# Keys and outputs of a scan turned by VectorE through memory scratch instead of by TensorE, in a gated scan-and-experts kernel

## The reference, cut to what is computed

```python
# x, ctx: (16, 256, 512)
k = layernorm(x); v = ctx
# per channel c, over the 256 steps of each of 16 sequences:
#   y_t = (e1*aa + e2*v_t) / (e1*bb + e2);  aa, bb decayed by exp(-exp(time_decay)), then exp(k_t)*v_t, exp(k_t) added
x = x + tanh(g_xattn) * y
h = layernorm(x)                                  # 4096 tokens
routed = two of eight experts per token (I=352), capacity 1280 rows each, weighted by the softmax of their two logits
shared = (silu(h @ Wg) * (h @ Wu)) @ Wd           # inner width 1408
x = x + tanh(g_ffn) * (routed + shared)
```

## Time and profile before

| | us |
|---|---|
| median of 3 runs | 1230.34 |
| lowest, highest | 1228.75, 1232.13 |
| the profiled execution | 1232.66 |
| its span, first to last instruction | 1230.9 |

### The profile page before, as it was taken

How to read it: one execution, slowest core, us unless ns; L and a number is a source line. 1 busy time by engine, 2 the same in 40 slices (tenths; PEclk the granted TensorE clock), 3 DMA queues, 4 the chain that set the end, 5 groups by cost and what they waited for, 6 DMA issues and landing times. The chain is left out here.

```text
span 1230.9 us, 25978 instructions
## 1 busy us (share of the span) xinstructions
PE 1163.2 (94%) x8396; PEld 817.2 (66%) x8396; DVE 682.7 (55%) x1357; ACT 509.6 (41%) x915; POOL 653.7 (53%) x754
## 2 busy tenths in 40 slices
PE   1478999999999999999999989999999999999998
PEld 1366777777777777777776767566666666666653
DVE  6776787786786777776777866222222223222112
ACT  5665444443544443544534443333333333333220
POOL 7887457367457457456557542344444444444320
PEclk9998999999999999999999989999999999999999
DMA  8373232232222222222332323999899989997738
GB/s 234 92 206 72 53 70 53 53 69 52 54 66 52 60 61 55 68 49 60 87 69 48 59 65 62 204 178 180 173 169 172 176 171 165 178 169 130 127 50 319
DMA packets 232773, 136.29 MB, mean 111 GB/s; under 512 B 176477, under 2 KB 201077, under 8 KB 232544
## 3 DMA queue, kind: packets, MB, share of 16 engines
q1 hardware_dynamic: 213792, 97.55, 34.3%
q0 software_dynamic: 18048, 37.47, 17.6%
q10 hardware_dynamic: 832, 0.02, 0.0%
HBM read 69.83 MB, written 44.97 MB: 93 GB/s over the span
## 5 line engine op out<-in xcount | busy, mean ns | idle before, releaser
L1024 PE MATMUL PU<-xT,wreg 128*128 128x256 f16 x4224 | 504.5, 276 | 0.4 <-DVE srng L1311 0.4
L1024 PEld LDWEIGHTS PU<-xT,wreg 128*128 128x128 f16 x4224 | 415.1, 99 | 74.8 <-DVE srng L1311 0.7
L753 POOL DMA_INDIRECT moe_d<-wkv,acc x71 | 112.0, 1578 | 217.2 <-ACT wkv L928 214.2
L1131 PE MATMUL PU<-acc,wkv 128*128 x1284 | 214.5, 312 | 0.0
L1057 PE MATMUL PD<-wreg,hreg 128*128 128x512 f16 x858 | 206.4, 379 | 0.0
L634 POOL TENSOR_TENSOR hreg<-srng,hreg 128x256 f16<-128x256 f32 x165 | 134.6, 822 | 73.9 <-ACT hreg L850 72.9
L1131 PEld LDWEIGHTS PU<-acc,wkv 128*128 128x128 f16 x1284 | 125.1, 97 | 69.4
L1545 DVE TENSOR_TENSOR wkv<-PR,wkv 128x384 f16<-128x384 f32 x71 | 39.6, 557 | 208.1 <-ACT wkv L922 148.7
L1152 PE MATMUL PD<-acc,wkv 128*128 (+1 forms) x639 | 149.6, 379 | 1.5 <-DVE wkv L1545 1.5
L834 ACT ACTIVATE srng<-PU 128x256 f32<-128x256 f32 x176 | 66.7, 379 | 201.4 <-PE PU L1024 149.5
L1057 PEld LDWEIGHTS PD<-wreg,hreg 128*128 128x128 f16 x858 | 84.0, 98 | 73.5
(11 more groups left out here) (177 smaller groups left out, 1327.5 us busy)
## 6 DMA issues: line engine op xcount, KB each, us to landing
wreg<-in_L_ffn_w_up_gate SPq DMA_DIRECT2D x48, 176.0 KB
acc<-in_x SPq DMA_DIRECT2D x32, 256.0 KB, 3.0
xhl_d<-wkv SPq DMA_DIRECT2D x32, 256.0 KB, 2.3
wkv<-in_ctx SPq DMA_DIRECT2D x112, 64.0 KB, 2.4
moe_d<-acc SPq DMA_DIRECT2D x13, 512.0 KB
out<-moe_d SPq DMA_DIRECT2D x2, 3328.0 KB, 21.1
acc<-n_L_ffn_shared_w_up_gate SPq DMA_DIRECT2D x16, 256.0 KB, 5.7
wreg<-in_L_ffn_w_down SPq DMA_DIRECT2D x12, 256.0 KB
```

Source lines behind the costliest of these rows:

```text
L753: pool.indirect_dma_start(out=moe_d, out_offset=bass.IndirectOffsetOnAxis(ap=didx[:, t:t + 1], axis=0), in_=ostage[t % 3], in_offset=None, ...
L1024: mm = pe.matmul(PU[r][:, gu * UN:(gu + 1) * UN], sU[:, m, gu, a, kt, :], xT[:, u.par, b, kt, :], start=(kt == 0 and a + b == 0), stop=(kt ...
L1131: mm = pe.matmul(up_set[t % 2][gu][:, 0:I], xgT[:, t % 4, a, kt, :], weights(h, ((gu * 2 + b) * KT + kt) * I, P, I), start=(kt == 0 and a ...
```

## The change

Three things change. First, for the 28 tiles of units 2 to 15, k and y are turned as v is. `norm_k` is followed by `store_k` (SP writes `kbuf`, 256 KB, to a scratch `k_d` in device memory), `load_k` (four 64 KB transfers back into `kbuf` with exchanged blocks) and `turn_k` on VectorE (`kbuf` into `PT`). After `divide` come `store_y` (to `y_d`), `load_y` (four transfers into `xln[k]`, the buffer that `norm_x2` later writes) and `turn_y` on VectorE. `den` of the next tile waits for the landing of `store_y` (semaphore `y_out`) where it waited for TensorE's turn. The tiles of units 0 and 1 keep the old stages and the old table, now `FIRST_AT`. Second, `STAGE_AT` has new steps for the others: the chain begins 3 to 4 steps earlier, and the tiles k=0 and k=1 are spread 3 to 7 steps apart. Third, routing steps move: 7 to 4 in odd units, 5 and 7 to 3 and 4 in even ones, and in unit 14 from 8 to 9.

```diff
+STAGE_AT = {
+    "stats_x": (-24, -20),
...
+    "turn_k": (-19, -16),
...
+    "turn_y": (-9, -6),
...
+            def store_k(c):
+                wait_alone(k_norm, c + 1)
+                sp.dma_start(k_d, kbuf).then_inc(k_out, 16)
+
+            def load_k(c):
+                wait_alone(k_out, 16 * (c + 1 - UT * PE_TURNED))
+                load_blocks(kbuf, k_d, k_in)
+
+            def store_y(c, k):
+                wait_alone(y_done, c + 1)
+                wait_alone(y_turned, c - 1)
+                sp.dma_start(y_d[k], y_of_nd).then_inc(y_out, 16)
+
+            def load_y(c, k):
+                wait_alone(xlo_ready, c - 1)
+                wait_alone(y_out, 16 * (c + 1 - UT * PE_TURNED))
+                load_blocks(xln[k], y_d[k], y_in)
...
                     for v, k in tiles_at("turn_k", u, s):
-                        turn_k(v, k)
+                        if turned_by_pe(v):
+                            turn_k(v, k)
...
                         for v, k in tiles_at("turn_y", u, s):
-                            turn_y(v, k)
+                            if turned_by_pe(v):
+                                turn_y(v, k)
...
+                else:
+                    wait_alone(y_out, 16 * (c - UT * PE_TURNED))
                 dve.tensor_tensor(nd[:, 0], v, nd[:, 1], ALU.mult).then_inc(d_used, 1)
...
+            def turn_k(c):
+                wait_alone(k_in, 64 * (c + 1 - UT * PE_TURNED))
+                dve.wait_ge(x2_done, c - 1)
+                dve.transpose(PT[:, :], kbuf).then_inc(k_turned, 1)
+
+            def turn_y(u, k):
+                c = u.tile(k)
+                wait_alone(y_in, 64 * (c + 1 - UT * PE_TURNED))
...
+                dve.transpose(PT[:, :], xln[k]).then_inc(y_turned, 1)
```

More of the change, by code:

```diff
@@ L72 @@
     "choose": (-6, 1),
+    "store_k": (), "load_k": (), "store_y": (), "load_y": (),
+}
+STAGE_AT = {
+    "stats_x": (-24, -20),
+    "norm_k": (-23, -19),
+    "store_k": (-23, -19),
+    "load_k": (-22, -18),
+    "turn_k": (-19, -16),
+    "exp_k": (-18, -14),
+    "factors": (-17, -13),
+    "turn_v": (-18, -13),
+    "load_v": (-17, -10),
+    "den": (-16, -12),
+    "num": (-15, -11),
+    "divide": (-14, -10),
+    "store_y": (-13, -9),
+    "load_y": (-12, -8),
+    "turn_y": (-9, -6),
+    "add_y": (-9, -6),
+    "norm_x2": (-7, -4),
+    "split_x": (-6, -3),
+    "logits": (-4, -1),
+    "choose": (-4, 3),
 }
@@ L131, with turned_by_pe @@
 LAST = [Route(GROUPS - 1, 14 * (GROUPS - 1), TILES - GT, UT, 0), Route(GROUPS, 14 * (GROUPS - 1) + 12, TILES - UT, UT, UT)]
+def turned_by_pe(u):
+    return u.fixed and u.v < PE_TURNED
 def tiles_at(stage, u, s):
-    return [(u.shift(-(o // JT)), k) for k, o in enumerate(STAGE_AT[stage])
-            if o % JT == s and u.shift(-(o // JT)).exists()]
+    found = []
+    for table, first in ((FIRST_AT, True), (STAGE_AT, False)):
+        for k, o in enumerate(table[stage]):
+            v = u.shift(-(o // JT))
+            if o % JT == s and v.exists() and turned_by_pe(v) == first:
+                found.append((v, k))
+    return found
 def key(u, s):
@@ L399, in load_x, with load_blocks @@
                 sp.dma_start(acc_tile(c), x_rows[bass.ds(c * P, P), :]).then_inc(x_in[u.par][k], 16)
+            def load_blocks(buf, rows, landed):
+                for q in range(P // SQ):
+                    sp.dma_start(buf[q * SQ:(q + 1) * SQ, :].rearrange("p (k b j) -> p k b j", k=KT, j=SQ),
+                                 rows.rearrange("(b i) (k q j) -> q i k b j", i=SQ, k=KT, j=SQ)[q]).then_inc(landed, 16)
+            def store_k(c):
[12 more added lines that the diff above has]
+                load_blocks(xln[k], y_d[k], y_in)
             def load_ctx(c, r):
@@ L451, in unit @@
                         start_sums(u.shift(-2))
-                    for v, k in tiles_at("turn_v", u, s):
+                    for v, k in tiles_at("store_y", u, s):
+                        store_y(v.tile(k), k)
+                    for v, k in tiles_at("load_k", u, s):
+                        load_k(v.tile(k))
+                    for v, k in tiles_at("load_y", u, s):
+                        load_y(v.tile(k), k)
+                    for v, k in tiles_at("load_v", u, s):
                         if v.shift(1).exists():
@@ L464, in unit @@
                             load_x(v.shift(2), k)
+                    for v, k in tiles_at("store_k", u, s):
+                        store_k(v.tile(k))
                     if key(u, s) in EARLY_LOAD_AT:
@@ L860, in unit @@
                         norm_k(v.tile(k))
[L861 removed]
+                    for v, k in tiles_at("exp_k", u, s):
                         exp_k(v.tile(k))
@@ L971, in turn_y @@
                 pe.wait_ge(y_done, c + 1)
[L972 to L976 removed]
+                pe.wait_ge(ek_ready, c + 2)
+                turn(PT, y_of_nd).then_inc(y_turned, 1)
             def logits(u, k):
@@ L1442, in unit @@
                             add_down(UT * (u.v - 2) + t, t, PD)
+                    for v, k in tiles_at("turn_y", u, s):
+                        if not turned_by_pe(v):
+                            turn_y(v, k)
                     for v, k in tiles_at("add_y", u, s):
@@ L1453, in unit @@
                         split_x(v, k)
+                    for v, k in tiles_at("turn_k", u, s):
+                        if not turned_by_pe(v):
+                            turn_k(v.tile(k))
                     for v, k in tiles_at("divide", u, s):
@@ L1464, in unit @@
                     for v, k in tiles_at("turn_v", u, s):
-                        if not (v.fixed and v.v < PE_TURNED):
+                        if not turned_by_pe(v):
                             turn_v(v, k)
```

40 lines of the change are left out of this document (21 added, 19 removed).

## The result

The changed kernel takes 1284.2 us (median of 5 runs, 1283.6 to 1287.2), the kernel before 1231.9 beside it; the ratio is 1.0434, 95% interval 1.0414 to 1.0453. I had forecast 1206, and gave 6 in 100 to slower.

What follows compares the result with a forecast made beforehand. TensorE, busy without idle time from 100 to 643 us, was taken as the bound. Terms -22.6 + 3 + 0 - 5 = -24.6 took 1232.7 to 1208.1 profiled, 1206 us median; forecast 1198 to 1211, range 1198 to 1220.

Steps and rivals of the forecast that it cites:

- TensorE's turns: Units 1 to 13: removing four turns a unit at 0.43 us each gives -22.6 us; a unit then takes 43.5 us.
- VectorE's turns: Each unit: four turns add 2.9 us to VectorE, which just fits, about 95% full; price 0.
- 76.3 us of waits: VectorE's waits for other engines in eleven units, 6.9 a unit, taken as room that leaves 2.3 us after the change.
- step 8 the heaviest: VectorE's step 8, a multiplication, split and divide, takes 5.0 us against 3.95, ends 1.1 us late, then catches up.
- a lag matters only from about 6 us: VectorE's lag stays near 1 to 3 us; TensorE feels it only from about 6 us, being three PU buffers ahead at most.
- Rival (c): VectorE becomes pacemaker through four waits for reloads; at 1.5 us each a unit takes 47.2 us, 1254 in all; 5 in 100.
- The way through memory: Stores and reloads of k and y through SP and DMA: +3 us, bounds 0 to 24.
- the tightest place: SP's DMA transpose of x for tile k=0, queued behind stores, reloads and landings, with 2.0 us of room before logits.
- The page's rule (e): Strided DMA 19 times slower: a reload of 61 us, some 2,500 us more, 3,700 in all; under 1 in 100.
- The beginning: End of unit 0: an earlier scan of unit 2 delays the split, hidden by the clearing if under 4 us; 0, bounds -2 to +8.
- Unit 14: Unit without "down": the second xT lands some 31 to 33 us after it begins instead of 38; -5 us, bounds -9 to +3.
- the condition that I gave for the upper bound: In unit 14, VectorE waits for y while everything queues behind; +3 us.

Runs made afterwards that it cites:

- d_sends: Changed kernel with split of tile 0 at step 4, choices at 5, norm of k of tile 1 at 4, slot transfers in steps 6 to 9; 1258.7 us.
- e_free: Like d_sends, but GpSimd's slot transfers two at step 8 and two in each of steps 2, 3 and 4 of the odd unit; 1246.0 us.
- f_pos9: e_free with TensorE's count of positions at step 9 of the odd unit rather than 8; 1250.5 us.
- x_nomem: Changed kernel without stores and reloads of k and y, VectorE turning kbuf and xln as they stand (y not right); 1268.3 us.
- x_pe_table: Changed kernel's new steps, but TensorE turns k from kbuf, and y after a plain read back; 1244.1 us.
- x_kbuf2: Changed kernel with k reloaded into a buffer of its own from unit 4 on; 1273.7 us.
- c_choices: Changed kernel with split of tile 0 at step 4, slot transfers two in each of steps 7 to 10, route_choices at step 5 not 4; 1280.0 us.
- x_split7: Changed kernel with only the split of tile 0 one step earlier, at step 4; 1279.9 us.

## Why the prediction was wrong

**TensorE's turns: right.** A unit without waits is 43.5 us, to a tenth (even units of d_sends, e_free, f_pos9). So the price of the turns on TensorE stands; no run had all 22.6 us of it.

**VectorE's turns: this step failed.** I priced them at 0, "because 2.3 us of waiting cover it". Three things are wrong in it. First, most of the 76.3 us of waits that I subtracted from, 51.4, were for ScalarE (and 9.6, put down to "issue", were for no engine that the view shows), and I treated them as slack. They are pieces of a loop of waits: in the chain above ScalarE waits for VectorE's turn and VectorE for ScalarE's silu. Instead of falling to 2 us a unit they grew by half, 51.4 to 76.4. Second, I took 43.5 / 11 for each step and the mean of the units, though the odd ones carry choices, positions and, on GpSimd, the tail of the slot transfers. I called step 8 the heaviest; what decides is the run from step 1 to step 5 of the odd unit, which begins with a divide that is late already and contains a turn of y, one of k and one of y again. Third, "a lag matters only from about 6 us" was meant for products of blocks, and TensorE does not wait for one in the changed kernel from 145.6 to 643 us; it does not hold for the split: `xT` of tile 0 has a date of its own, and TensorE asks for it two steps after the split. What it costs, instead of 0: without any way through memory VectorE's turns at these steps give 1268.3 (x_nomem), and TensorE's at the same steps 1244.1 (x_pe_table) although TensorE has 1.74 us a unit more. So the turns on VectorE cost some 24 us or more, one of the two times being a single execution, and some 47 with TensorE's share as an estimate (24 and the forecast's 22.6). The 40 us between the changed kernel and x_pe_table hold the way through memory as well.

Rival (c) named the right engine and the right sign, with too small a size (47.2 us a unit and 1254; the mean of units 2 to 11 is 48.6, the time 1284), and had 5 in 100. The waits for reloads that it gave as cause are not in VectorE's list from 145.6 to 643 us; the one wait for memory there, 2.5 us, is for the stored y.

**The way through memory: a mis-sized term, and a wrong reason.** I took +3 of 0 to 24; x_nomem says 16. SP is not late at the tightest place: it issues 0.3 us after the split. What the 16 are made of stays open. The 10 us that a second buffer gives back (x_kbuf2) are no part of them that one could subtract: it shortens the even units by 2.4 us and lengthens the odd ones by 1.4, while x_nomem, which keeps the single buffer, shortens the odd ones by 1.4 and leaves the even ones nearly as they were. But it shows that the single `kbuf`, of which I wrote that it leaves room, has a price: some 5 us over units 2 to 12 in that one execution.

The page's rule (e) fell: a quarter of a reload, 64 KB in runs of 128 bytes, lands in 2.6 us. By that rule of the Trainium skill, "VectorE: DVE Perf Modes", section "The three transpose paths", a reload would have been an estimated 61. The page says so of a large innermost stride at the destination; `load_blocks` writes runs of 32 neighbouring words, so I had stretched the rule to a case that it does not name.

**The beginning**: 0 forecast, +3.7 measured, within the bounds. The transpose is issued at 94.2 and not at 86.9: the split itself stands at 93.5 and not at 86.1, 7.4 us later, more than the 4 us that the clearing would have hidden.

**Unit 14**: -5 forecast with +3 as the bound, and it lasts 42.0 us against 38.3, so +3.7. Here the condition that I gave for the upper bound came true, and the time went beyond it: VectorE waits 2.96 us for the reloaded y with the split behind it, after 3.92 us for a silu, and TensorE stands 8.87 us. Without the way through memory what follows unit 13 is 3.1 us shorter (x_nomem). Unit 13, which I counted as one like the others, adds 6.0.

**The clock** had no term at all. In the two units shown the waits are followed by matmuls at the lower clock, which costs 1.7 us behind the wait of 2.06 and 2.2 behind the one of 4.95: 3.9 of the 11 us that these two units are longer than 43.5 each.

My first theory fell as well. That the steps alone were to blame, whoever turns, is refuted by x_pe_table; that VectorE alone was, whatever the steps, by e_free, which keeps all four turns on it and gives back 38 of the 52 us. It takes both: VectorE's 2.9 us more, and a table in which they stand in the odd unit's full half. What stays open: whether some other table carries all four turns below 1231 us, what the extra cost of the choices at step 5 (c_choices) is made of, and how much of the odd unit GpSimd's hold on VectorE takes (last section).

## What to carry to other kernels

Waits of an engine in a pipeline of engines that feed one another are not free time: before work is moved onto it, follow for one whole period what each of its neighbours' queues holds behind the operation that it delays, and take the fullest unit and not the mean. A transfer with a date of its own (here the split before `logits`) must be looked at apart from the ring that tolerates a lag. And price a new wait of TensorE with the clock behind it.

## What the runs showed that I had not expected

A short wait can cost nearly double: 2.06 us of waiting and then 1.7 us at the lower clock. A wait of 4.95 us costs 2.2 more, hardly more than the short one. A shorter one costs no more than itself: in x_kbuf2 TensorE waits 1.17 us in an even unit of 44.8 us, and the 15 matmuls behind it take 1.64 us, as at full clock.

A tiny operation on VectorE can take 2.5 us. `wexp<-topv`, 4 elements a partition, has a mean of 146 ns in the changed kernel and of 2545 (five of them) in f_pos9, where it meets GpSimd's pair of 128x512 multiplications; VectorE, then GpSimd:

```profile
314.92 2.52 DVE L1468 TENSOR_TENSOR wexp<-topv 128x4 f32 x1 [0.21 <-issue]
```
```profile
314.75 0.68 POOL L702 TENSOR_TENSOR hreg<-srng,hreg 128x256 f16<-128x256 f32 x1
315.38 1.04 POOL L663 TENSOR_TENSOR wkv<-wkv,e 128x512 f32<-128x512 f32 x1
316.38 1.03 POOL L667 TENSOR_TENSOR wkv<-wkv,e 128x512 f32<-128x512 f32 x1
```

It ends with the second of them. In x_split7 the same fell on `ohx<-ohx,ohs` (mean 809 ns against 162), and in f_pos9 also on `wexp<-wexp` in another step (1013 against 164). By its means the kernel before has it too (`ohx<-ohx,ohs`, 388 ns). Which operation is hit changes with the steps of the table, some 2 to 2.4 us in an odd unit; no run here takes GpSimd's pair away to show it. The Trainium skill, "SBUF — State Buffer", section "SBUF: two separate sides", has a rule for it: VectorE and GpSimd share one pair of ports under an exclusive lock when a VectorE operation has two inputs there. `wexp<-topv` and `ohx<-ohx,ohs` have two such inputs, and that they are held agrees with it. `wexp<-wexp` has one input, so that clause does not cover it. And by the page the lock is for one instruction, while `wexp<-topv` is held through three of GpSimd's in a row, from L702 on; that part the rows show and the rule does not say.
